# Loads of three stages issued ahead of their layer norms, and the first contexts of the attention over grams normalised beside its queries

## The reference, cut to what matters

```python
x = x + tanh(g_xattn[0]) * xattn0(layernorm(x), ctx)      # parts 0 and 1
x = x + tanh(g_ffn[0])   * ffn0(layernorm(x))             # ternary weights, low-rank path
...
# part 4, the attention over grams: no softmax, so out = qn (kn^T v)
Qn, Kn, Vn = layernorm(Q, ln1_g, ln1_b), layernorm(K, ...), layernorm(V, ...)
qn, kn = l2norm(heads(Qn @ wq)), l2norm(heads(Kn @ wk))    # 16 heads of 64
x1 = Q + (qn kn^T) v @ wo + bo
out = x1 + gelu(layernorm(x1, ln2_g, ln2_b) @ w1 + b1) @ w2 + b2
# parts 5 and 7, the one-matrix mixtures: softmax router over 8 experts, top 2 / top 1,
# y = sum_e weight_e * (x @ W_e)
```

## Time and profile before

| | us |
|---|---|
| median of 3 runs (lowest, highest) | 6163.29 (6157.67, 6165.86) |
| the profiled execution's own time | 6152.64 |
| its span, first to last instruction | 6150.5 |
| mean granted TensorE clock | 0.936 of full |
| busy: DVE / ACT / POOL | 4466.4 / 3193.4 / 1844.2 |

### The profile page before, as it was taken

How to read it: one execution, slowest core, us unless ns; L and a number is a source line. 1 busy time by engine, 2 the same in 40 slices (tenths; PEclk the granted TensorE clock), 3 DMA queues, 4 the chain that set the end, 5 groups by cost and what they waited for, 6 DMA issues and landing times. The chain is left out here.

```text
span 6150.5 us, 133121 instructions
## 1 busy us (share of the span) xinstructions
PE 5287.2 (86%) x51447; PEld 3802.1 (62%) x51447; DVE 4466.4 (73%) x9168; ACT 3193.4 (52%) x6024; POOL 1844.2 (30%) x1456
## 2 busy tenths in 40 slices
PE   1888989888669999989839999999999749999997
PEld 1777777777258888877824444444444427888885
DVE  6898898986357777763457777777777547777776
ACT  0666666666246666652224444444444216666663
POOL 4777676772022222211001111111111022222220
PEclk6999999999689999999969999999999869999998
DMA  4555565553167777743010000000000048888981
GB/s 107 124 131 126 127 129 125 131 125 80 37 122 140 140 140 139 140 81 115 24 31 21 16 15 15 15 15 15 15 15 10 7 91 151 163 161 161 161 155 30
DMA packets 368544, 545.53 MB, mean 89 GB/s; under 512 B 115780, under 2 KB 248006, under 8 KB 367606
## 3 DMA queue, kind: packets, MB, share of 16 engines
q1 hardware_dynamic: 365894, 533.81, 42.9%
q0 software_dynamic: 2048, 3.67, 0.2%
HBM read 413.45 MB, written 123.90 MB: 87 GB/s over the span
## 5 line engine op out<-in xcount | busy, mean ns | idle before, releaser
L653 DVE CUSTOM_DVE_ANT_0 attn_logits<-attn_scores,attn_shift 112x750 f32<-112x750 f32 x1024 | 944.9, 932 | 440.3 <-PE attn_scores L457 440.0
L569 ACT ACTIVATE attn_probs_t<-attn_pt 125x448 f32<-125x448 f32 x1536 | 829.6, 541 | 581.7 <-PE attn_pt L472 561.1
L472 PEld LDWEIGHTS attn_pt<-ident,attn_logits 112*125 112x125 f32 x6144 | 851.6, 189 | 179.7 <-issue 92.8
L472 PE MATMUL attn_pt<-ident,attn_logits 112*125 112x112 f32 x6144 | 920.7, 273 | 26.4 <-ACT attn_logits L560 24.8
L2246 PE MATMUL attn2k_pk<-attn_wk,attn2k_cn_t 128*125 128x512 f32 x1536 | 738.8, 603 | 53.0 <-ACT attn2k_cn_t L2317 36.7
L2257 PE MATMUL attn2k_pg<-attn2k_kn,attn2k_cn 125*128 125x512 f32 x1536 | 725.0, 594 | 6.0 <-ACT attn2k_gram L2325 3.9
L2412 DVE TENSOR_REDUCE attn2k_ss<-attn2k_sq 125x16 f32<-125x1024 f32 x384 | 466.9, 1216 | 257.7 <-ACT attn2k_sq L2354 257.6
L386 POOL CAST attn_k_parts<-xn_t 128x500 bf16<-128x500 f32 x192 | 199.3, 1038 | 1422.6 <-DVE xn_t L623 1422.6
L2354 ACT ACTIVATE attn2k_sq<-attn2k_pk 125x1024 f32<-125x1024 f32 x384 | 391.5, 1019 | 324.8 <-PE attn2k_pk L2246 324.6
L1165 ACT ACTIVATE attn_probs_t<-attn_pt 125x448 f32<-125x448 f32 x768 | 413.8, 539 | 275.0 <-PE attn_pt L1053 273.0
L2246 PEld LDWEIGHTS attn2k_pk<-attn_wk,attn2k_cn_t 128*125 128x125 f32 x1536 | 273.1, 187 | 416.7 <-issue 320.8
(11 more groups left out here) (363 smaller groups left out, 10434.9 us busy)
## 6 DMA issues: line engine op xcount, KB each, us to landing
attn_k_packed<-k_scratch SPq DMA_DIRECT2D x384, 375.0 KB, 6.4
attn_k_packed<-k_scratch SPq DMA_DIRECT2D x384, 187.5 KB, 4.4
k_scratch<-attn_k_parts SPq DMA_DIRECT2D x64, 1125.0 KB, 7.6
attn_ctx_t<-in_ctx_t SPq DMA_DIRECT2D x64, 750.0 KB, 7.4
k_scratch<-attn_k_parts SPq DMA_DIRECT2D x96, 375.0 KB, 3.7
attn_ctx_t<-in_ctx_t SPq DMA_DIRECT2D x96, 250.0 KB, 4.1
attn2k_ctx<-in_ctx SPq DMA_DIRECT2D x32, 750.0 KB
attn_mask_in<-in_mask SPq DMA_DIRECT2D x192, 109.4 KB
```

Of the source, the lines that this page charges most:

```text
L472: last = pe.transpose(pt[(3 * at + t) % 2][0:KC, (c % 4) * PAIR:(c % 4 + 1) * PAIR], logits[:, at % 3, c * KC:(c + 1) * KC], g.ident[0:PAI ...
L569: act.activation(probs_t[0:KC, p // 4, 4 * t:4 * t + 4, (p % 4) * PAIR:(p % 4 + 1) * PAIR], pt[(3 * at + t) % 2][0:KC, 0:QUAD].rearrange(" ...
L653: dve.tensor_tensor_reduce(out=logits[:, at % 3, cols].rearrange("p (b k) -> p b k", b=2), in0=scores[h][0:PAIR, :, 0:QTR], in1=shift[:, n ...
```

## The change

`ffn0`, `attention2` and `mixture` take a function `ahead`, which is their norm. They allocate their SBUF tiles and semaphores, call `fetch`, call `ahead()`, and then allocate PSUM and open their own block, which no longer holds the loads:

```diff
 def ffn0(nc, g, a, ahead):
+        fetch(nc, loads, loaded)                 # six DMAs
+        ahead()
 def mixture(..., b_experts, ahead):
+        fetch(nc, [(wr..), (order..), (br..)], loaded)
+        fetch(nc, [(we..)] + ([] if b_experts is None else [(be..)]), experts_in)
+        ahead()
 def attention2(nc, g, a, ahead):
+        fetch(nc, [(wv_t..), (wo..), (wq..), (wk..), (bo..)], loaded)
+        fetch(nc, [(gain..), (shift..)], const_in)
+        fetch(nc, [(ctx[:, 0, :, :], a["ctx"][0]...)], ctx_even)
+        ahead()
```

In `attention2` all tiles and semaphores of attn2k but PSUM now belong to the outer scope, the query stage's own get names with `q_`, and the steps for the first contexts move into the block of attn2q:

```diff
 # attn2q's block
+                @block.gpsimd
+                def _(pool):
+                    pool.wait_ge(const_in, 32)
+                    context_affine(pool, 0, 0)
                 @block.scalar
                 def _(act):
+                    context_root(act, 0)
+                    context_normed(act, 0, 0, range(CH))
                     for half in range(2):
                         act.wait_ge(vo_ready, half + 1)
                         ...                                # copy to w_vo
                 @block.vector
                 def _(dve):
+                    for step in range(4):
+                        context_stats(dve, 0, 0, 0, step)
+                    context_scales(dve, 0)
                     chain = Chain(dve, q_steps)
 # attn2k's block
                     def load(n, j, half):
+                        if is_first(n):
+                            return
                         wait(sp, raw_ready, (n - 1) * CH)
-                    root(0)
-                    normed(0, 0, range(CH))
                     turned(0, 0)
-                    for step in range(4):
-                        stat(0, 0, 0, step)
-                    scales(0)
```

The block `loads` ahead of part 4's norm becomes a `fetch` without a wait; the norm's ACT waits for the two vectors where it first uses them (second round, first quad), and their semaphore is cleared, with a barrier, after the part:

```diff
-                    loads(nc, "ln1", ((twice[0], a["ln1_g"]), (twice[1], a["ln1_b"])))
-                    norm(nc, g, f"norm{n}", gate=gate, twice=(twice[0][:], twice[1][:]))
-                    part()
+                    landed = nc.alloc_semaphore("ln1_landed")
+                    fetch(nc, [(twice[0][:], a["ln1_g"]), (twice[1][:], a["ln1_b"])], landed)
+                    part(lambda: norm(nc, g, f"norm{n}", gate=gate, twice=..., twice_in=landed))
+                    nc.clear_and_free_semaphores([landed])
+                    nc.all_engine_barrier()
```

More of the change, by code:

```diff
@@ L219, in _ @@
                         affine = only_y or (rd and twice)
+                        if twice_in is not None and rd and q == 0:
+                            act.wait_ge(twice_in, 32)
                         if not affine:
@@ L1481, in ternary, with _, ffn0 @@
         chain(dve.tensor_scalar(wi, wi, scale[:, i:i + 1], None, ALU.mult))
-def ffn0(nc, g, a):
+def fetch(nc, pairs, landed):
+    with nc.Block() as block:
+        @block.sync
+        def _(sp):
+            for dst, src in pairs:
+                sp.dma_start(dst, src).then_inc(landed, 16)
+def ffn0(nc, g, a, ahead):
     r = scope(nc, "ffn0")
@@ L1596, in mixture @@
         values = lambda t: py[t % 3][0:PAIR, :, :].rearrange("p a (e d) -> p (a e) d", d=D)
-        with nc.Block() as block:
[L1598 to L1605, removed]
+        fetch(nc, [(wr[:], w_router), (order[:], a["c_order"].partition_broadcast(PAIR)),
+                   (br[:], b_router.partition_broadcast(PAIR))], loaded)
+        fetch(nc, [(we[:], w_experts.rearrange("e h d -> h e d"))] + ([] if b_experts is None else [(be[:], b_experts)]),
+              experts_in)
+        ahead()
+        pl, pb = r.ps("pl", [128, TILES, E]), r.ps("pb", [128, 512])
+        py = [r.ps(f"py{i}", [128, 2, 512]) for i in range(3)]
+        with nc.Block() as block:
             @block.tensor
@@ new lines, in attention2 @@
+        ctx_in = (ctx_even, ctx_odd)
+        loaded = whole.sem("loaded")
+        fetch(nc, [(wv_t[:], a["wv2_t"].rearrange("(h r) c -> r h c", r=DH2)),
+                   (wo[:], a["wo2"].rearrange("(h r) c -> r h c", r=DH2)), (wq[:], a["wq2"]), (wk[:], a["wk2"]),
+                   (bo[:], a["bo2"])], loaded)
+        fetch(nc, [(gain[:], a["ln1_g_row"].partition_broadcast(KC)),
+                   (shift[:], a["ln1_b_row"].partition_broadcast(KC))], const_in)
+        fetch(nc, [(ctx[:, 0, :, :], a["ctx"][0].rearrange("(c p) d -> p c d", p=KC))], ctx_even)
@@ new lines, in attention2, with context_stats @@
+        ahead()
+        def context_stats(dve, n, j, half, step):
+            if step < 3:
+                if step == 0:
+                    dve.wait_ge(ctx_in[j], half * 16 + 16)
+                    wait(dve, steps, n * 3)
+                for c in range(4 * step, 4 * step + 4):
+                    last = dve.bn_stats(stats[:, c, :], ctx[:, j, c, :])
+                if step == 2:
+                    last.then_inc(steps, 1)
+                return
+            dve.wait_ge(steps, n * 3 + 1)
+            wait(dve, scale_ready, n)
+            dve.sem_inc(held, 1)
+            for c in range(CH):
+                last = dve.bn_aggr(mv[:, c, :], stats[:, c, :])
+            last.then_inc(steps, 1)
+            dve.wait_ge(steps, n * 3 + 2)
+            dve.tensor_scalar(var[:], mv[:, :, 1], EPS, None, ALU.add).then_inc(var_ready, 1)
@@ L2279, in out @@
                         last.then_inc(y_ready, 1)
-                    pe.wait_ge(const_in, 32)
                     turn(0, 0, 0)
@@ L2607, in program @@
                     part()
+            elif n % 2:
+                part(lambda: norm(nc, g, f"norm{n}", gate=gate))
             else:
```

190 lines of the change are left out of this document (76 added, 114 removed).

## The result

The changed kernel took 6104.09 us (median of 4 runs, 6102.23 to 6115.17), the kernel before beside it 6164.57 us: a ratio of 0.9905, with a 95% interval from 0.9887 to 0.9922, or 60 us less. The forecast was 27 less, with 6124 as its lower end. The sign was right and the size was not. The kernel before was profiled once; stage times are compared with that one trace.

A forecast was written before the change was run, and what follows sets the result against it. Seams where no engine runs were taken to bound the kernel, not TensorE's 86% busy time. Terms -1.7 - 1.8 + 7.7 + 0.4 - 10.3 + 3.1 - 25.6 + 1.5 gave -26.7 us: median 6136, range 6124 to 6149.

The forecast's parts named there:

- Part 1, -1.7: Part 1's start: 5.2 us of waiting go, 3.0 of issues and 0.5 of block end are added; net -1.7 us.
- Mixtures, -1.8: Parts 5 and 7: waits of 3.4 and 4.35 us go, issues and block ends added; -0.7 and -1.05, together -1.8 us.
- Rival B: Mixtures: shorter PE idle lets router products run at full clock, 3 us less in each; -33 us, 6130; chance 8%.
- Ahead of part 4's norm, +7.7: Part 4: fetch issues and block ends now precede the norm, which begins 7.7 us later (-2.0 + 5.7 + 1.2 + 0.8 + 2.0).
- the 2.0 that I put on a held issue of contexts: Ahead of part 4's norm: contexts' issue held behind 2 MB of weights, taken as 2.0 us, bounds 0 and 8.3.
- the rule that I weighed against the rows and set aside: Part 4's fetches: issues would take about 0.45 us each, and part 4 gain some 4 us more than forecast.
- Queries, -10.3 and +3.1: Part 4's queries: wait for weights gone, -10.3 us; ACT doing contexts first delays the first query product, +3.1, bounds 2 and 4.
- Keys, -25.6: Part 4's keys: statistics come at 10.0 instead of 35.55 us, after DVE waits for sequence 1's contexts; -25.6, bounds -28.7 and -23.9.
- Clock, +1.5: Part 4's keys: PE stands some 4 us in its second chunk, so products run slow; +1.5 us, bounds 0 to 4.
- The loop, 0: Part 4's loop over contexts: 14 rounds with unchanged bodies, given no term in the sum.
- Rival C: Loop over contexts: rounds lie elsewhere in the instruction stream, each losing 3.73 us at half clock; +52, 6188; chance 3%.
- What I had said would show it: Signs in the changed profile: immediate block starts, norm 7 to 8 us later, contexts' issue over 0.4 us, DVE standing some 3.

The follow-up runs named there:

- b_small: Kernel before with only part 1 and the mixtures changed, loop at 6745; profiled once, only stages read: rounds of 98.0 us, 2.4 us less to part 1's first turned weight.
- a_third: The changed kernel unaltered, run again on another chip beside the kernel before: ratio 0.9923 (0.9909 to 0.9936).
- a_again: The changed kernel unaltered, run once more on another chip against the kernel before: ratio 0.9918 (0.9901 to 0.9934).

## Why the forecast was wrong

**Part 1, -1.7.** Right: -2.1 in the profiled pair, -2.4 in `b_small`. What came behind it, 17.8 us at half clock, I had not thought of; it comes without the change as well.

**Mixtures, -1.8.** Near it at the two starts, -1.6 (part 5's sum should have been -0.6, since four issues and two block ends are 2.8). In part 5 the time from the norm's first row to the router products fell from 17.26 to 14.12 us and 2.9 were added ahead: -0.3. In part 7 21.2 us became 19.9: -1.3. Rival B did not come: the products took 6.11 us. But in the whole stretch behind the last y of part 4 the gain does not show. That stretch took 1319.5 to 1321.7 us in the four kernels with the mixtures as before, 1319.4 to 1324.6 in the twelve with fetch blocks, and only without such blocks less, 1312.4 and 1313.2.

**Ahead of part 4's norm, +7.7.** Wrong by 3.9: it was +3.8. The five weights with their block end took 3.7 us (forecast 5.7), since `bo` was not held, with the order of the five turned round; gain, shift and the contexts took 1.2 and 0.85 as forecast; the 2.0 that I put on a held issue of contexts were nought. I carried over a hold from a row without asking what was queued in which order, and the order was new in the diff. By the rule that I weighed against the rows and set aside (the Trainium skill, "DMA: Bandwidth & Descriptors", "Anatomy of one DMA", which speaks of another issuing path) many descriptors can be emitted before their generation shows. The trace of the changed kernel agrees with it, with 0.27 to 0.80 us an issue, while the run with the old order (2.37 us for `bo`) shows the row to be right for its own order.

**Queries, -10.3 and +3.1.** Right: 31.96 to 21.29 us is -10.7, and the first query product came 10.10 us behind the first `w_vo` product instead of 7.12, +3.0, with ACT's copies behind the contexts as foreseen. **Keys, -25.6.** Right: 35.55 to 9.31, -26.2, DVE's stand 2.38 us where I said 3. **Clock, +1.5.** Right as far as it can be told: from those statistics to the first y 73.4 us became 74.9: +1.5.

So part 4's start is -28.8 where the steps gave -23.6 (with 0.4 at the end to come), and 3.9 of that difference are the holds.

**The loop, 0.** This is the step that failed. I took the 14 rounds as unchanged because their body is ("long pipelines that the change leaves alone") and gave them no term in the sum; they measured -18.1 us. Rival C named the very mechanism, the loop's place in the instruction stream, but looked at PE, priced it at a group of products on half clock, and gave it one sign: a loss, from a state taken to be free of it, at 3%. PE's wait at a round's start, on which C rested, is 1.14 us in the changed kernel as well:

```profile
3412.62 1.98 PE L2302 MATMUL attn2k_pk<-attn_wk,attn_cn_t 128*125 128x512 f32 x4 [1.14 <-ACT attn_cn_t L2368]
```

The kernel before was the one that paid, on DVE. Its trace showed it, in the row of 14.9 us in 13 waits on 'issue' and in 50 code packets in ten rounds, and I had read neither; the waits of DVE in the loop would have made "may lose" into "pays over 1 us a round now, and may stop paying". Which places are free of it that trace could not say. -18.1 us, on top of a forecast gap of 27, is the larger part of the miss, and the 3.9 us of the holds the smaller. That the change moved the loop to a free place and not to a worse one was luck: with one fetch block instead of three, at 6741, nearly the same change was worth 8 us. And the profiled pair looks nearer to the forecast (-37 against -27) than it was, because the 17.8 us of part 1 stand against the loop's 18.1.

**What I had said would show it** came out: DVE and the router products at their blocks' start, PE's transpose within 0.3 us, some 3 us ahead of the first L2124's counterpart, DVE's stand of 2.38 us. The norm at 7 to 8 us later and the contexts' issue over 0.4 us did not.

The rest of the 60 us is spread. On the chip of `a_third` the gap was 44.4 by medians: 29.4 stay with the loop at its old place, 15.0 go. By two profiles with like hidden layers (before and `a_again`) it is 44.5: 27.7 from part 3's end to the first y, 17.8 in the loop, less 1.0 elsewhere. What made the first comparison's median 60 was not seen in any trace: of the changed kernel's four runs the profiled one stands 10 us above the rest, which would fit a slow hidden layer there alone, but the others were not profiled. The four comparisons named at the start (the last with sixteen increments more) gave 60, 52, 44 and 40 us; forecast, loop and holds together are 49.

## What to carry to other kernels

Before costing an edit ahead of a long loop, look in the loop for waits on 'issue' and for instruction packets: if there are some, the loop's place costs time each round, and any edit ahead of it, even two empty instructions, can move the result by more than the edit is worth (here from -18 to +24 us on the kernel before, for 288 instructions on DVE). Compare variants only at the same class of place, and pad when they are not, where the engine waits anyway: 122 empty instructions in part 1 left no trace, 112 at the end of a block cost 10 us. Loads that are to run under a norm belong inside the norm's own block; a block for them costs its issues and its end in front of everybody (7.0 us less wait ahead of part 4's norm without it). And a held issue in a trace is a fact of the order in which its neighbours were queued: ask what the new order is.

## What the runs showed of the hardware

- With DVE's loop of 288 instructions at some places five packets of 8 KB of code came in each round, and at others none: none at 6743, 6745, 6747 and 6761; 5 a round at 6739, 6741, 6857 and 6867. The price was 1.4, 3.0 to 3.3, 0.4 and 1.4 us a round.
- Empty instructions on DVE alone brought these packets and took them away, and in ten rounds (3500 to 4500 us) of the kernels at 6743, 6745, 6747 and 6761 no code packet came for any engine.
- An empty increment at the end of DVE's block held the others up by 10.1 us for 112 of them and 0.85 for 16.
- PE's hidden layer in part 1 has a shorter and a longer time, some 15 us apart, with no difference in the program: in the profiled pair the granted clock stayed at 0.50 for 30 us longer.
- On two of the chips part 3 took some 30 us longer than on the others in each kernel profiled there (from the table load for its exponential to part 4's first product 394 to 409 us against 364 to 379), with waits of ACT in that part of up to 21.9 us, put down to a DMA, that the others do not show. The cause was not looked for.
